# One product for denominators and numerators, expert logits inside the value product, and rank sums on GpSimd, in a two-layer attention and mixture-of-experts kernel

## What is computed

```python
# layer 0, attention: linear attention with 16 heads of 8
q_feat = elu(rope(q) * SCALE) + 1;  k_feat = elu(rope(k)) + 1
kv = einsum('bhtd,bhtv->bhdv', k_feat, v);  k_sum = k_feat.sum(axis=2)
denom = maximum(einsum('bhtd,bhd->bht', q_feat, k_sum), 1e-06)
out = einsum('bhtd,bhdv->bhtv', q_feat, kv) / denom[..., None]
# layer 0, experts: 64 experts of width 64 in 8 groups, 8 chosen from 4 groups, and a shared one
# layer 1, attention: messages of 4 neighbours through silu, and softmax over the 8 best keys
local = mean_w(silu([x_t, x_(t-w)] @ Wm1 + bm1) @ Wm2 + bm2)
scores = (q @ k.T) / sqrt(D), causal, 8 best kept;  glob = softmax(scores) @ v
y = concat([local, glob]) @ Wo + bo
# layer 1, experts: 8 experts of width 256, the best two of softmax(xn @ gate_w.T)
result = sum_k weight_k * (silu(xn @ w1.T) * (xn @ w3.T)) @ w2.T
```

## Time and profile before

| | |
|---|---|
| median of 3 runs | 1878.09 us (1873.88 to 1881.1) |
| the profiled execution | 1875.96 us, of which its span is 1874.2 us |
| PE busy | 1766.2 us, 94% of the span |
| DVE busy | 1362.1 us, 73% |
| ACT busy | 808.8 us, 43% |
| POOL busy | 539.1 us, 29% |
| mean granted TensorE clock | 0.989 of full speed |

### The profile page before, as it was taken

One profiled execution on the slowest core, in us unless ns is written; L12 is line 12 of the kernel. 1 busy time (PEld: TensorE's weight loads), 2 busy tenths in 40 slices (PEclk: granted clock), 3 DMA queues, 4 the chain that ended last, 5 costly groups with the idle time before them and its releaser, 6 DMA issues.

```text
span 1874.2 us, 25718 instructions
## 1 busy us (share of the span) xinstructions
PE 1766.2 (94%) x7678; PEld 1257.3 (67%) x7678; DVE 1362.1 (73%) x3946; ACT 808.8 (43%) x1421; POOL 539.1 (29%) x527
## 2 busy tenths in 40 slices
PE   2888999999999999999999999999999999999995
PEld 2655777677777777777777767767767676766663
DVE  4775878777777777777777777878786868555557
ACT  3432535353535353535353535353445444454431
POOL 0102050404131322222222313140404043366670
PEclk9998999999999999999999999999999999999998
DMA  6767272636354554535454636262736354566869
GB/s 195 174 192 206 68 182 70 175 77 161 91 136 116 117 135 101 150 91 151 96 143 95 157 81 171 67 178 64 173 74 171 71 130 119 187 222 203 259 212 300
DMA packets 166440, 269.84 MB, mean 144 GB/s; under 512 B 13656, under 2 KB 52440, under 8 KB 166048
## 3 DMA queue, kind: packets, MB, share of 16 engines
q1 hardware_dynamic: 157728, 250.50, 51.2%
q0 software_dynamic: 8576, 17.70, 3.0%
HBM read 202.21 MB, written 65.93 MB: 143 GB/s over the span
## 4 chain that ended last, share of the span: by engine, by line
PE 71%; DVE 9%; issue 8%; DMA 4%; POOL 4%; ACT 2%; SPq 1%; POOLq 0%; DVEq 0%; ACTq 0%
PE ps_y L608 19%; PE ps_gate L553 6%; PE ps_up L553 6%; PE ps_gate L555 6%; PE ps_up L555 6%; PE ps_gate L554 6%; PE ps_up L554 6%; POOL y_kept L1406 3%; DVE silu_h L810 2%; PE ps_side L554 2%; PE ps_side L555 2%; PE ps_side L553 2%; PE ps_side L574 2%; DVE msg L1106 2%; PE ps_y L634 2%
## 5 line engine op out<-in xcount | busy, mean ns | idle before, releaser
L810 DVE TENSOR_TENSOR silu_h<-ps_up,silu_h 128x512 f32<-128x512 f32 x618 | 425.4, 688 | 431.1 <-ACT silu_h L1215 356.0
L1215 ACT ACTIVATE silu_h<-ps_gate 128x512 f32<-128x512 f32 x618 | 365.9, 597 | 444.7 <-PE ps_gate L555 440.3
L608 PE MATMUL ps_y<-silu_h,w_dn 128*128 128x512 f32 x1056 | 540.5, 593 | 0.0
L804 DVE TENSOR_TENSOR silu_h<-coef_b,silu_h 128x512 f32<-128x512 f32 x528 | 367.5, 696 | 19.8 <-DMA coef_b<-coef_kept 17.3
L553 PE MATMUL ps_gate<-xnT,w_gu 128*128 128x512 f32 x528 | 290.0, 549 | 0.2 <-ACT silu_h L1215 0.2
L1433 POOL TENSOR_TENSOR msg<-msg 128x512 f32<-128x512 f32 x48 | 61.8, 1288 | 650.7 <-ACT msg L1345 650.6
L608 PEld LDWEIGHTS ps_y<-silu_h,w_dn 128*128 128x128 f32 x1056 | 199.1, 189 | 50.5 <-issue 7.7
L553 PE MATMUL ps_up<-xnT,w_gu 128*128 128x512 f32 x528 | 209.2, 396 | 17.2 <-DVE silu_h L810 17.2
L555 PE MATMUL ps_gate<-xnT,w_gu 128*128 128x512 f32 x528 | 208.7, 395 | 0.0
L555 PE MATMUL ps_up<-xnT,w_gu 128*128 128x512 f32 x528 | 208.1, 394 | 0.0
L554 PE MATMUL ps_gate<-xnT,w_gu 128*128 128x512 f32 x528 | 207.7, 393 | 0.0
(11 more groups left out here) (254 smaller groups left out, 2827.3 us busy)
## 6 DMA issues: line engine op xcount, KB each, us to landing
coef_b<-coef_kept SPq DMA_DIRECT2D x256, 512.0 KB, 6.7
slots_x<-empty SPq DMA_DIRECT2D x15, 2080.0 KB, 14.0
w_block<-w_kept SPq DMA_DIRECT2D x45, 512.0 KB, 4.7
xs<-slots_x SPq DMA_DIRECT2D x37, 260.0 KB, 3.0
y_back<-y_kept SPq DMA_DIRECT2D x15, 512.0 KB, 6.9
w_raw<-in_ffn_w SPq DMA_DIRECT2D x49, 128.0 KB, 2.6
w_down<-in_ffn_w SPq DMA_DIRECT2D x45, 128.0 KB, 4.6
xres<-in_x SPq DMA_DIRECT2D x16, 256.0 KB, 3.1
```

Source lines behind the costliest of these rows:

```text
L608: eng.matmul(ps_y[:, :], w_dn[:, j], silu_h[:, g % HBUFS], start=j == 0, stop=last).then_inc(pe_down)
L804: eng.tensor_tensor(silu_h[:, s], coef_b[:, q % COEF_RING, k], silu_h[:, s], ALU.mult).then_inc(dve_h)
L810: eng.tensor_tensor(silu_h[:, s], ps_up[g % 2][:, :], silu_h[:, s], ALU.mult).then_inc(dve_h1)
L1215: eng.activation(silu_h[:, s], ps_gate[g % 2][:, :], ACT.Silu).then_inc(act_silu)
```

## The change

The change has four parts.

1. den and num become one product with 144 columns. It is issued in two halves, one per sequence, as num0 (tile 19) and num1 (tile 20). den_inv and mix become mix0 (tile 20) and mix1 (tile 21), each of them a maximum, a reciprocal and a multiplication over half the width. mixT moves from tile 21 to 22.
2. The eight logit columns are appended to the value weights. logit1 and v1 become vl0 and vl1 (both tile 10), twelve products of 136 columns. top1 copies the logits from two banks, and v1 on ACT, now at tile 11, copies the values in two halves after that.
3. A new step prefix on POOL (tile 29; tile 16 in ROUTE1_LAST) adds the marks of the blocks one after another into gbefore, by a copy and three additions of 128x8 that wait for one another. rank on PE is then two products of 40 columns, and it waits for prefix.
4. Steps move: score_exp from tile 12 to 10; q1, k1, s0, s0_mask, s1, s1_mask, top, strike0, strike1 and attend_exp one tile later each; near, self and add1 to add4 one tile earlier each.

```diff
 ATTENTION0 = [(0, "kv0"), (1, "kv1"), (2, "kv2"), (3, "kv3"), (4, "k_rope"), (5, "q"), (6, "q_cos"), (6, "q_swap"), (7, "q_sin"), (8, "q_min"),
-              (12, "feat_exp"), (13, "q_feat"), (14, "k_feat"), (16, "kvsum"), (17, "kvmask"), (18, "den"), (19, "den_inv"), (19, "num"),
-              (20, "mix"), (21, "mixT")]
+              (12, "feat_exp"), (13, "q_feat"), (14, "k_feat"), (16, "kvsum"), (17, "kvmask"), (19, "num0"), (20, "num1"), (20, "mix0"),
+              (21, "mix1"), (22, "mixT")]
-ROUTE0 = [(0, "stats0"), (2, "norm0"), (4, "xT0"), (5, "x_lo0"), (8, "logit0"), (12, "score_exp"), (13, "sigmoid0"), (16, "sigmoid1"),
+ROUTE0 = [(0, "stats0"), (2, "norm0"), (4, "xT0"), (5, "x_lo0"), (8, "logit0"), (10, "score_exp"), (13, "sigmoid0"), (16, "sigmoid1"),
-ROUTE1 = [(5, "stats1"), (7, "norm1"), (8, "xT1"), (9, "x_lo1"), (10, "logit1"), (11, "top1"), (13, "gate_exp"), (23, "softmax"), (28, "select"),
-          (30, "rank"), (31, "key"), (32, "first2"), (33, "slot"), (34, "send0"), (35, "send1"), (36, "send2"), (37, "send3"),
+ROUTE1 = [(5, "stats1"), (7, "norm1"), (8, "xT1"), (9, "x_lo1"), (10, "vl0"), (10, "vl1"), (11, "top1"), (13, "gate_exp"), (23, "softmax"), (28, "select"),
+          (29, "prefix"), (30, "rank"), (31, "key"), (32, "first2"), (33, "slot"), (34, "send0"), (35, "send1"), (36, "send2"), (37, "send3"),
           (39, "send4"), (40, "send5"), (41, "send6"), (42, "send7")]
...
-ROUTE1_LAST = [(5, "stats1"), (7, "norm1"), (8, "xT1"), (9, "x_lo1"), (10, "logit1"), (11, "top1"), (13, "gate_exp"), (14, "softmax"), (15, "select"),
-               (17, "rank"), (18, "key"), (19, "first2"), (20, "slot"), (20, "table"), (21, "send0"), (21, "send1"), (22, "send2"), (22, "send3"),
+ROUTE1_LAST = [(5, "stats1"), (7, "norm1"), (8, "xT1"), (9, "x_lo1"), (10, "vl0"), (10, "vl1"), (11, "top1"), (13, "gate_exp"), (14, "softmax"), (15, "select"),
+               (16, "prefix"), (17, "rank"), (18, "key"), (19, "first2"), (20, "slot"), (20, "table"), (21, "send0"), (21, "send1"), (22, "send2"), (22, "send3"),
...
-ATTENTION1 = [(10, "q1"), (11, "k1"), (12, "s0"), (13, "s0_mask"), (13, "s1"), (14, "s1_mask"), (15, "top"), (16, "strike0"), (17, "strike1"),
-              (18, "attend_exp"), (19, "v1"), (21, "sum0"), (22, "sum1"), (23, "p0"), (24, "p1"), (24, "near"), (25, "self"), (26, "mixa"),
-              (26, "add1"), (27, "mixa_add"), (27, "add2"), (28, "add3"), (29, "add4"), (31, "mixl"), (32, "mixl_add")]
+ATTENTION1 = [(11, "v1"), (11, "q1"), (12, "k1"), (13, "s0"), (14, "s0_mask"), (14, "s1"), (15, "s1_mask"), (16, "top"), (17, "strike0"), (18, "strike1"),
+              (19, "attend_exp"), (21, "sum0"), (22, "sum1"), (23, "p0"), (23, "near"), (24, "p1"), (24, "self"), (25, "add1"), (26, "mixa"),
+              (26, "add2"), (27, "mixa_add"), (27, "add3"), (28, "add4"), (31, "mixl"), (32, "mixl_add")]
...
 TAKES = {"xT0": "x_lo0", "logit0": "score_exp", "coefT": "coefT", "kv0": "kv0", "kv1": "kv1", "kv2": "kv2", "kv3": "kv3",
-         "q": "q_cos", "q_swap": "q_sin", "kvsum": "kvmask", "den": "den_inv", "num": "mix", "mixT": "mixT", "yT": "y_add", "fold": "fold_lo",
-         "xT1": "x_lo1", "logit1": "top1", "rank": "key", "q1": "q1", "k1": "k1", "s0": "s0_mask", "s1": "s1_mask", "v1": "v1", "p0": "p0",
+         "q": "q_cos", "q_swap": "q_sin", "kvsum": "kvmask", "num0": "mix0", "num1": "mix1", "mixT": "mixT", "yT": "y_add", "fold": "fold_lo",
+         "xT1": "x_lo1", "vl0": "v1", "vl1": "v1", "rank": "key", "q1": "q1", "k1": "k1", "s0": "s0_mask", "s1": "s1_mask", "p0": "p0",
...
-                elif what == "den":
+                elif what in ("num0", "num1"):
+                    s, wide = int(what[3]), P + HEADS
                     eng.wait_ge(*read("kvsum", key))
                     eng.wait_ge(pool_qfeat, key + 1)
-                    for r in range(ROWS):
-                        ins = eng.matmul(ps[:, r * HEADS:(r + 1) * HEADS], qf[:, r * P:(r + 1) * P], kv[:, r // 2, P:], start=True, stop=True)
-                    ins.then_inc(signal)
-                elif what == "num":
-                    for r in range(ROWS):
-                        ins = eng.matmul(ps[:, r * P:(r + 1) * P], qf[:, r * P:(r + 1) * P], kv[:, r // 2, 0:P], start=True, stop=True)
+                    for i, r in enumerate(pair(s)):
+                        ins = eng.matmul(ps[:, i * wide:(i + 1) * wide], qf[:, r * P:(r + 1) * P], kv[:, s], start=True, stop=True)
                     ins.then_inc(signal)
                 elif what == "mixT":
-                    eng.wait_ge(dve_mix, key + 1)
+                    eng.wait_ge(*read("num0", key))
+                    eng.wait_ge(*read("num1", key))
...
-                elif what == "logit1":
+                elif what in ("vl0", "vl1"):
+
+                    s, wide = int(what[2]), P + EXPERTS1
                     eng.wait_ge(*read("xT1", key))
                     eng.wait_ge(*read("fold", 0))
-                    for r in range(ROWS):
-                        at, mine, w = r * 2 * EXPERTS1, row(halves1(), r), w1[:, :, 5 * P:]
-                        eng.matmul(ps[:, at:at + 2 * EXPERTS1], mine[0], w, start=True, stop=False)
-                        ins = eng.matmul(ps[:, at:at + EXPERTS1], mine[1], w[:, 0], start=False, stop=True)
+                    for i, r in enumerate(pair(s)):
+                        ins = mm3(ps[:, i * wide:(i + 1) * wide], row(halves1(), r), (w1[:, 0, 4 * P:], w1[:, 1, 4 * P:]))
                     ins.then_inc(signal)
                 elif what == "rank":
 
                     eng.wait_ge(dve_sel, key + 1)
+                    eng.wait_ge(pool_before, (ROWS + 1) * (key + 1))
                     eng.matmul(ps[:, 0:(ROWS + 1) * EXPERTS1], neg_before, flat(gsel[:, :, :]), start=True, stop=False)
-                    for r in range(ROWS):
-                        ins = eng.matmul(ps[:, (r + 1) * EXPERTS1:(ROWS + 1) * EXPERTS1], neg_ones,
-                                         gsel[:, r].unsqueeze(1).to_broadcast([P, ROWS - r, EXPERTS1]), start=False, stop=r == ROWS - 1)
-                    ins.then_inc(signal)
+                    eng.matmul(ps[:, 0:(ROWS + 1) * EXPERTS1], neg_ones, flat(gbefore[:, :, :]), start=False, stop=True).then_inc(signal)
...
...
-                elif what == "den_inv":
-                    eng.wait_ge(*done("den", c))
-                    eng.tensor_scalar(den_inv[:, :], side_bank("den", c)[:, 0:ROWS * HEADS], EPS_DEN, None, ALU.max).then_inc(read("den", c)[0])
-                    eng.wait_ge(*read("den", c))
-                    keep(eng.reciprocal(den_inv[:, :], den_inv[:, :]))
-                elif what == "mix":
-                    by_head = [P, ROWS * HEADS, HEAD]
-                    eng.wait_ge(*done("num", c))
-                    wait_own()
-                    eng.tensor_tensor(mix_rows[:, :].rearrange("p (h d) -> p h d", d=HEAD), side_bank("num", c)[:, :].rearrange("p (h d) -> p h d", d=HEAD),
-                                      den_inv[:, :].unsqueeze(2).to_broadcast(by_head), ALU.mult).then_inc(read("num", c)[0])
-                    eng.wait_ge(*read("num", c))
-                    eng.sem_inc(dve_mix, 1)
+                elif what in ("mix0", "mix1"):
+                    s = int(what[3])
+                    ps = side_bank(f"num{s}", c)[:, 0:2 * (P + HEADS)].rearrange("p (r n) -> p r n", r=2)
+                    inv = den_inv[:, s * 2 * HEADS:(s + 1) * 2 * HEADS]
+                    eng.wait_ge(*done(f"num{s}", c))
+                    keep(eng.tensor_scalar(inv.rearrange("p (r h) -> p r h", r=2), ps[:, :, P:], EPS_DEN, None, ALU.max))
+                    wait_own()
+                    keep(eng.reciprocal(inv, inv))
+                    wait_own()
+                    eng.tensor_tensor(mix_rows[:, s * SEQ:(s + 1) * SEQ].rearrange("p (r h d) -> p r h d", r=2, d=HEAD),
+                                      ps[:, :, 0:P].rearrange("p r (h d) -> p r h d", d=HEAD),
+                                      inv.rearrange("p (r h) -> p r h", r=2).unsqueeze(3).to_broadcast([P, 2, HEADS, HEAD]),
+                                      ALU.mult).then_inc(read(f"num{s}", c)[0])
...
                 elif what == "top1":
-                    logits = side_bank("logit1", c)[:, 0:ROWS * 2 * EXPERTS1].rearrange("p (r n e) -> p r n e", r=ROWS, n=2)
-                    eng.wait_ge(*done("logit1", c))
-                    keep(eng.tensor_copy(gate[:, :, :], logits[:, :, 0]))
-                    wait_own()
-                    eng.tensor_tensor(gate[:, :, :], logits[:, :, 1], gate[:, :, :], ALU.add).then_inc(read("logit1", c)[0])
-                    eng.wait_ge(*read("logit1", c))
+                    for s in range(SEQS):
+                        logits = side_bank(f"vl{s}", c)[:, 0:2 * (P + EXPERTS1)].rearrange("p (r n) -> p r n", r=2)[:, :, P:]
+                        eng.wait_ge(*done(f"vl{s}", c))
+                        eng.tensor_copy(gate[:, 2 * s:2 * s + 2], logits).then_inc(dve_logit1)
```

(23 more changed lines are left out.)

35 lines of the change are left out of this document (18 added, 17 removed).

## The result

The changed kernel takes 1965.38 us (median of 4 runs, 1961.77 to 1966.16), the kernel before beside it 1879.28 us: ratio 1.046, 95% interval 1.0445 to 1.0474. The forecast was 1908 us with a range of 1868 to 1926. The direction and both new waits were foreseen; the size was not.

A forecast was written before the change was run, and what follows sets the result against it. PE was taken to bound the kernel on average, with DVE, ACT and POOL setting the stretch from K to rank. The profiled 1876 us plus 15 of work and waits plus 17 of clock gave 1908 us, range 1868 to 1926.

The forecast's parts named there:

- The clock: After the new wait at rank the granted clock falls to 1.2 GHz in 10 of 15 chunks, 1.7 us each: +17 us.
- The rival with a fall in every chunk: Waits as forecast, and the clock falls behind rank's wait in all 15 chunks, +26 us: 1917 us; chance 12%.
- Second new wait: rank behind prefix.: PE waits about 3.5 us at rank for POOL's prefix, queued behind the last message add; K to rank grows 2.4 us.
- The rival with POOL's small instructions at 0.73 us: The small POOL additions of prefix run slow, +1.9 us per chunk, and the clock falls always: about 1940 us; chance 6%.
- The rest of the chunk stays on PE: -0.67 (rank), -0.76 (mixl), +0.44: Outside K to rank: six rank passes go, mixl's wait goes, merged logit and value products move in at 1.34 for 0.90.
- 0.3 of small waits: Small PE waits near tiles 14 to 16 that a later K hides, taking a chunk's growth from 1.4 to 1.1 us.
- the cover that might go: At s0 (tile 13) ACT has kT ready some 0.6 us ahead; without that PE waits up to 1 us per chunk.
- First new wait: mixT behind mix1.: PE reaches mixT at K+15.3 but DVE ends mix1 at K+17.1, so PE waits 1.7 us there.
- The signs.: Expected profile: chunk of 97 to 99 us, waits at rank and mixT, none at mixl or num0; wrong if period 92.

The follow-up runs named there:

- busy_wait: The changed kernel with five useless products of 512 columns on PE ahead of rank's wait; ratio 1.0294 to the kernel before, period 99.83 us.
- merge_prefix: merge_only with the rank sums on POOL, prefix at tile 29 and the message adds where the kernel before has them; ratio 1.012 to the kernel before.
- merge_only: The kernel before with the first part of the change alone (num0, num1, mix0, mix1, mixT at tile 22); ratio 0.9892 to the kernel before.
- prefix_28: The changed kernel with prefix at tile 28 in place of 29, ahead of POOL's last message add; ratio 1.0055 to the kernel before.
- mixT_23: The changed kernel with mixT at tile 23 in place of 22; ratio 1.0396 to the kernel before.
- after_last: The changed kernel with gbefore placed behind all other buffers, which keep their addresses of the kernel before; ratio 1.0474 to the kernel before.
- after_aligned: The changed kernel with gbefore padded to 192 bytes, later buffers as divisible by 64 as before; ratio 1.0458 to the kernel before.
- best24: merge_only plus near, self, adds one tile earlier, rank sums on POOL, gbefore padded to 192 bytes, select at tile 24, prefix at 25; ratio 0.9846, 1849.75 us.

## Why the prediction was wrong

A chunk grew by 6.1 us. I had +1.1 us of work and waits and 1.2 of clock (17 us over 14 chunks), 2.3. The missing 3.8 us lie in three steps.

- **"The clock. … I take a fall in 10 of the 15 chunks, +17 us; the ends are 0 and 15, 0 and +26."** This step failed most: it is 2.6 us in each of 14 chunks, 36 us, shown by busy_wait. I priced a fall with the one in chunk 0, 3.4 us at the half clock, 1.7 us of full speed lost. Here a fall lasts 6.8 us, begins while PE still stands, and lies for 5.5 us on products. My upper end of 26 us was no bound, since it rested on that one row. The same trace of the kernel before held two longer waits, with longer low stretches around their ends:

```profile
51.00 0.80 PE L553 MATMUL ps_up<-xnT,w_gu 128*128 128x512 f32 x1 [5.91 <-DVE silu_h L810]
...
157.44 0.80 PE L553 MATMUL ps_up<-xnT,w_gu 128*128 128x512 f32 x1 [8.40 <-DVE silu_h L810]
```

```profile
47.00:54.50 7.50, 3.50 (x8) 2.18 (x9) 4.61 (x13) 1.47 (x5) 0.00 (x0) 0.54 1.08 231
154.00:163.50 9.50, 6.06 (x16) 4.17 (x17) 4.92 (x14) 3.55 (x9) 0.00 (x0) 0.50 1.07 225
```

The prediction's "the trace agrees for the wait of 3.59 us alone" overlooked them, and its low stretch of 3.4 us was the shortest of three. The rival with a fall in every chunk had the mechanism right, the same price and hence the same fault. Of the Trainium skill, TensorE: Matmul & The Clock Gate, section "HAM oscillation — how this bites in real kernels", the text said that by its rule the fall comes in all chunks; for the wait of 4.26 us the trace agrees, in all 14; for 2.85 us (merge_prefix) the fall came in 9 of 14 only.
- **"Second new wait: rank behind prefix."** The mechanism and nearly all its distances hold: from add1 to add4 4.23, 3.89 and 3.93 us for 4.2, 3.9 and 3.9, and PE stood behind POOL's last message add. The term was mis-sized: add1 came at K+27.5 (27.1), and prefix took 2.04 us (1.1, with bounds of 1.0 and 3.2), its copy 0.70 us. I had argued that DVE has little to do while PE stands; it had times_coef and times_up to do, right beside the copy. Rank starts at K+44.5 and not K+43.1, the wait is 4.26 us and not 3.5: +1.4 us. The working that puts PE there at K+39.6 is not given; it was K+40.2. The rival with POOL's small instructions at 0.73 us came nearest (1940 us): the copy did take 0.70, the three additions 0.42 each.
- **"The rest of the chunk stays on PE: -0.67 (rank), -0.76 (mixl), +0.44"**, less 0.3 of small waits. This made -1.3 us; at the full clock (busy_wait) it is 55.31 us from rank to K against 55.58, -0.3: another +1.0 us. Tiles 10 to 16 grew by 1.03 us where I had 0.44 less 0.3: the s0 wait of 0.3 us came, which I named as the cover that might go ("up to 1 us per chunk") but costed at nothing, and nothing shows the 0.3 that I took off for small waits. That leaves some 0.3 us of these tiles unexplained. And 0.3 us in tiles 32 to 9 come from the addresses, which I had not thought of at all.
- **"First new wait: mixT behind mix1."** Right: 1.7 us forecast, 1.83 measured in the chunk shown, mix1's product starting at K+16.9. Both ends of it came 0.3 us later than counted, so the size is no luck. (By its own figures, K+17.1 less K+15.3, the wait was 1.8.) merge_only shows what I did not say: this wait belongs to the second and fourth parts of the change and hardly to the merged product, which alone gains 1.1%.
- **The signs.** The waits at den and mixl went, num0 does not wait, and the period is not 92. The removed work was real where it can be seen by itself: tiles 17 to 20 fell by 2.84 us (den and v1; I had 3.2), rank's tile by 0.7 (prefix_28: 4.09 less its wait of 1.15, against 3.66). It came back as waits, since DVE, ACT and POOL set the stretch from K to rank.

By the same sum with these sizes: 1876 + 15 + 36 (clock) + 20 (1.4 us x 14 at rank) + 14 (1.0 x 14, the rest) = 1961 us; the profiled execution took 1961.8. The last term is the remainder of the 6.1 us per chunk, so this sum shows that the 14 chunks hold the whole loss, and no more than that. The range failed by the clock term, since its top of 1926 us held every fall at 1.7 us.

Still open: which property of the addresses costs the 0.02 to 0.04 us per tile, what the unexplained 0.3 us of tiles 10 to 16 are, and why one and the same wait at rank is followed by a fall in some chunks and by none, or a shorter one, in others (merge_prefix, mixT_23).

## What to carry to other kernels

When a product is moved out of a tensor engine's stretch that other engines set, its time is not won but turned into a wait, and a long wait costs more than itself (here 4.26 us and 2.6 more): price the low clock behind it from a run in which the wait is filled with useless products, not from one fall seen elsewhere. A step handed to another engine is put behind whatever that engine's queue holds, so place it in that queue first (here one number in a table, 4% of the time). Before judging the parts of a bundle, time one part alone: the first part of this change gained 1.1%, hidden in a bundle that lost 4.6%.

## What the runs showed of the hardware that was not expected

- A wait of 4.26 us brought about 6.8 us at 1.2 GHz in every chunk, the fall beginning inside the wait. With 2.85 us, the same in every chunk of merge_prefix, 9 of 14 chunks had a fall (0.79 over 8 us) and the others none (1.00). With waits of 1.83 us at mixT and 1.15 us at rank (prefix_28) the steady chunks had none.
- A low stretch cost half of what of it lay on products: 2.6 us for 5.5 (busy_wait against the changed kernel), 1.65 us for 3.4 (two chunks of merge_prefix), 0.4 us for 0.8 (after_last). What lay on the wait cost nothing.
- The changed kernel, after_aligned and after_last have one period, 102.4 us, though their tiles differ by 0.5 us. Work saved at the full clock came back as a longer tile at the low one.
- An unused buffer of 160 bytes per partition made the kernel before 0.33% slower by moving the buffers behind it, the expert weights among them.
- GpSimd's copy of 128x8 took 0.70, 0.19 and 0.45 us (changed kernel, prefix_28, best24); the three dependent additions took 1.26, 1.09 and 0.77 us together. Where a times_coef of DVE, with both inputs in SBUF, ran beside the copy, the copy ended 0.05 us behind it (753.49 against 753.44 in the changed kernel, 697.58 against 697.53 in best24); where none did, it took 0.19.
